# Two-layer transformer block on eight cores: a constant loaded first, an output projection in two parts, and the last feed-forward's norm and quantisation moved into the last head pair of attention

## What is computed

```python
def _L0_attn_ref(hidden_states, Wq, Wk, Wv, Wo):
    ...                                       # q, k: 16 heads of 16; v: 16 heads of 64
    A = jnp.tril(jnp.einsum('bhnf,bhmf->bhnm', taylor_exp(q), taylor_exp(k)))
    y = jnp.einsum('bhnm,bhme->bhne', A, v)   # divided by the row sums of A
    return y.transpose(0, 2, 1, 3).reshape(b, l, N_HEADS * V_DIM) @ Wo

def _L0_ffn_ref(x, w_gate, w_up, w_down):     # hidden 3072, int weights
    return (silu(x @ wg.T) * (x @ wu.T)) @ wd.T

def _L1_attn_ref(x, Wq, bq, Wk, bk, Wv, bv, Wo, bo, global_indices):
    ...                                       # 16 heads of 64, blocks of 64 tokens
    final = out_local + out_gk                # softmax over 3 blocks + softmax over 2 global blocks
    final = final.at[:, :, global_indices].set(out_rows)   # the two global blocks see all tokens
    return ctx @ Wo.T + bo

def _L1_ffn_ref(x, w1, conv_w, conv_b, w2):   # hidden 4096
    h = bit_linear(x, w1)                     # activations rounded to 8 bits by row, weights to -1, 0, 1
    h = silu(depthwise_conv1d(h))
    return bit_linear(h, w2)

x = x + _L0_attn_ref(_layernorm(x), ...)
x = x + _L0_ffn_ref(_layernorm(x), ...)
x = x + _L1_attn_ref(_layernorm(x), ...)
x = x + _L1_ffn_ref(_layernorm(x), ...)
```

## Time and profile before

| | |
|---|---|
| median of 3 runs | 2296.45 us (2292.74, 2296.45, 2488.86) |
| profiled execution, its own time | 2293.34 us |
| its span, slowest core (core 5) | 2291.8 us |
| spans of the eight cores | 2278.8 to 2291.8 us |
| PE busy | 1955.2 us (85%) |
| DVE, ACT, POOL busy | 1167.9, 1101.0, 28.7 us |

### The profile page before, as it was taken

The page is one execution under the profiler, slowest core; times in us unless marked ns, Lnnn a source line. Parts: engine busy times, 40 slices in busy tenths (PEclk is TensorE's granted clock), DMA queues, the critical chain, the costliest instruction groups (busy, mean ns, idle before and its releaser), DMA issues. The chain is left out here.

```text
span 2291.8 us, 35064 instructions; the slowest of 8 cores (2278.8 to 2291.8 us)
## 1 busy us (share of the span) xinstructions
PE 1955.2 (85%) x12314; PEld 911.1 (40%) x12314; DVE 1167.9 (51%) x2092; ACT 1101.0 (48%) x1994; POOL 28.7 (1%) x72
## 2 busy tenths in 40 slices
PE   3699999887899995999988888777893699979999
PEld 1334333323344442444444444444441344434444
DVE  2322656424535521521646666666556588875442
ACT  2477676754411100111225777677544788864221
POOL 0000000000000000000000000000000000000000
PEclk8799999868899997999999999788796699989999
DMA  7101545500087604622001000000101222241332
GB/s 191 30 1 38 168 162 169 119 2 1 1 212 225 215 28 83 203 63 46 1 1 29 11 11 11 11 11 2 38 1 75 83 74 74 74 136 57 111 118 85
DMA packets 64746, 170.12 MB, mean 74 GB/s; under 512 B 4416, under 2 KB 37184, under 8 KB 57664
## 3 DMA queue, kind: packets, MB, share of 16 engines
q1 hardware_dynamic: 58208, 134.31, 17.2%
q0 software_dynamic: 6368, 33.56, 8.4%
HBM read 167.85 MB, written 33.55 MB: 88 GB/s over the span
## 5 line engine op out<-in xcount | busy, mean ns | idle before, releaser
L671 PE MATMUL f0R<-lnT,wgu 128*128 128x512 bf16 x1536 | 336.0, 382 | 26.6 <-DMA wgu<-f0wgu_d 26.6
L431 ACT ACTIVATE a0bq<-a0S 128x1024 bf16<-128x1024 f32 (+1 forms) x320 | 268.8, 894 | 117.2 <-PE a0S L355 116.6
L671 PEld LDWEIGHTS f0R<-lnT,wgu 128*128 128x128 bf16 x1536 | 151.3, 99 | 210.9 <-issue 32.6
L706 ACT ACTIVATE f0si<-f0R 128x1024 bf16<-128x1024 f32 x48 | 49.2, 1025 | 386.6 <-PE f0R L671 386.6
L1305 PE MATMUL g1hp<-g1q1T,g1t 128*128 128x512 bf16 x1024 | 225.6, 381 | 5.4 <-DVE g1a L1425 4.0
L1329 PE MATMUL g1hp<-g1t,g1q1T 128*128 128x512 fp8e4 x1024 | 222.7, 381 | 2.1 <-ACT g1q1T L1380 2.1
L732 DVE TENSOR_TENSOR f0hT<-f0si,f0R 128x1024 bf16<-128x1024 bf16 x48 | 58.6, 1222 | 225.2 <-PE f0R L671 225.2
L1102 ACT ACTIVATE a1pt<-a1T 128x768 bf16<-128x768 bf16 (+2 forms) x152 | 118.6, 787 | 113.2 <-PE a1T L987 103.6
L372 PE MATMUL a0y<-a0bq,a0vv 128*64 128x512 bf16 (+3 forms) x640 | 128.4, 396 | 28.1 <-DVE a0yT L511 18.3
L1305 PEld LDWEIGHTS g1hp<-g1q1T,g1t 128*128 128x128 fp8e4 x1024 | 98.4, 98 | 132.4 <-issue 19.6
L1329 PEld LDWEIGHTS g1hp<-g1t,g1q1T 128*128 128x128 bf16 x1024 | 100.5, 98 | 124.1 <-issue 4.4
(11 more groups left out here) (189 smaller groups left out, 2947.9 us busy)
## 6 DMA issues: line engine op xcount, KB each, us to landing
a0wst<-g1w_d SPq DMA_DIRECT2D x64, 512.0 KB, 4.1
f0wst<-g1w_d SPq DMA_DIRECT2D x32, 1024.0 KB, 5.9
hs_scr<-g1hsp SPq DMA_DIRECT2D x32, 512.0 KB, 3.2
...
```

Source lines behind the costliest of these rows:

```text
L431: s.activation(bq[:, u % 4, :, n0:512], sS[:, u % 2, :, n0:512], AF.Square).then_inc(s_sq, 1)
L671: mm = t.matmul(R[:, k % 4, 512 * n2:512 * (n2 + 1)], wgu[:, cc % 3, x, j, :], lnT[:, j, t0 + 512 * n2:t0 + 512 * (n2 + 1)], start=(j == 0 ...
```

## The change

It has three parts.

1. Layer-0 attention's start: SP loads `a0qb` before x. The statistics run four tiles ahead instead of two, DVE also writes the negated mean (`neg`), and ACT itself makes `a0nb` from it; `a0lsc` has four buffers and the transposes use four PSUM banks.
2. Layer-0 output projection: `W` items carry a fourth field, the half of the heads. The halves over pairs 0 to 3 (32 items of 4 matmuls each, added to `xs`) are filled into pair 6 and the first two batches of pair 7, one or two in a batch; `finish` keeps the halves over pairs 4 to 7 (4 matmuls each). `wo` is loaded in two parts.
3. Norm and quantisation of the last feed-forward's input move into pair 7 of layer-1 attention: `finish(k)` there puts `Z` (row maximum and rounding of the tile before, DVE; back to bf16, now on POOL), `W`, `Q` (transposes two tiles back) and `N` (statistics on DVE, normalised tile on ACT). In pair 7, POOL takes over DVE's scaling in `X` and ACT takes over the write of `a1yT` in `V`. Part of the ternary weight `t1` (12 of 32 chunks) is loaded during attention, with a layout by chunk. The old stage in `emit_l1ffn` and its helper functions are gone.

```diff
@@ a0_order
+    first = [("W", ti, n2, 0) for ti in range(NT) for n2 in range(2)]
...
-        out.extend([("W", ti, 0), ("W", ti, 1)])
+        out.extend([("W", ti, 0, 1), ("W", ti, 1, 1)])
...
+        if 120 <= k < 142:
+            for _ in range(1 + k % 2 * (k < 140)):
+                out.append(first.pop(0))
@@ emit_l0attn, POOL and SP
-                g.wait_ge(s_pj, A0_PIECES * 4)
-                g.dma_start(wo[:, :, :], wo_d).then_inc(s_wo, 16)
+                for x in range(2):
+                    g.wait_ge(s_pj, A0_PIECES * (3 + x))
+                    g.dma_start(wo[x][:, :, :], wo_d[:, 4 * x:4 * x + 4, :]).then_inc(s_wo[x], 16)
...
+                sp.dma_start(qb[:, :], qb_d).then_inc(cstd, 16)
                 for g in range(8):
...
-                sp.dma_start(qb[:, :], qb_d).then_inc(cstd, 16)
@@ PE
-                        if ti >= 2:
-                            t.wait_ge(N1.ev, ti - 1)
-                        norm_pe_transpose(t, N1, lsc, ident, as_tiles(sS[:, ti % 2, 0, :]), ti)
+                        if ti >= 4:
+                            t.wait_ge(N1.ev, ti - 3)
+                        norm_pe_transpose(t, N1, lsc[:, ti // 2 % 2 * 2:, :], ident, as_tiles(lnp(ti)), ti)
...
-                        t.wait_ge(s_y, 29 + ti // 4)
-                        for j in range(ND):
+                        t.wait_ge(s_y, 29 + ti // 4 if x == 1 else 16)
+                        for j in range(4):
@@ ACT
-                            s.wait_ge(s_nb, ti // 2 + 1)
-                        if ti >= 2:
-                            s.wait_ge(N1.tp, ti - 1)
+                            s.drain()
+                            for i in range(ti, ti + 2):
+                                s.activation(nb[:, i:i + 1], N1.rstd[:, i:i + 1], AF.Copy,
+                                             scale=neg[:, i:i + 1])
+                            s.drain()
+                        if ti >= 4:
+                            s.wait_ge(N1.tp, ti - 3)
@@ a1_order
+    done = list(range(1, NT)) + [0]
+
+    def finish(k):
+        if k >= 1:
+            out.append(("Z", k - 1, done[k - 1]))
+        out.extend([("W", done[k], 0), ("W", done[k], 1)])
+        if k >= 2:
+            out.append(("Q", k - 2, done[k - 2]))
+        out.append(("N", k, done[k]))
...
         elif i < len(items) and m >= 5:
-            out += [("W", m - 4, 0), ("W", m - 4, 1)]
-    out += [("W", ti, n2) for ti in (13, 14, 15, 0) for n2 in range(2)]
-    return out
+            finish(m - 5)
+    for k in range(12, NT):
+        finish(k)
+    return out + [("Q", 14, done[14]), ("Z", 15, done[15]), ("Q", 15, done[15])]
@@ emit_l1attn, POOL: items X of pair 7, and Z
+                        g.wait_ge(s_rr, m + 1)
+                        if m < 16:
+                            for u in range(1 if m == 0 else 0, 2):
+                                lo = 64 if u == 0 else 0
+                                g.tensor_scalar(pp[:, m % 2, u, lo:lo + 192], pp[:, m % 2, u, lo:lo + 192],
+                                                rr[:, m % 2, 0, u:u + 1], None, ALU.mult)
+                                x = g.tensor_scalar(pp[:, m % 2, u, 256:384], pp[:, m % 2, u, 256:384],
+                                                    rr[:, m % 2, 1, u:u + 1], None, ALU.mult)
+                        else:
+                            x = g.tensor_scalar(pr_[:, :], pr_[:, :], rr[:, 2, 0, 0:1], None, ALU.mult)
+                        x.then_inc(s_p7, 1)
...
+                        g.tensor_scalar(q1c[:, k % 2, :], lx[k % 2].bitcast(I32)[:, :], am[:, ti:ti + 1],
+                                        1.0 / 127.0, ALU.mult, ALU.mult).then_inc(N.ap, 1)
@@ SP
+                sp.wait_ge(s_av, use(4, 0))
+                sp.dma_start(t1[:, 0:12, :, :], t_d[0, :, 0:12288].rearrange("p (c j d) -> p c j d", c=12, j=ND)
+                             ).then_inc(l_t1[0], 16)
@@ ACT: item N
+                        norm_act_rstd(s, N, k, ti, 1)
+                        s.drain()
+                        s.activation(nb[:, ti:ti + 1], N.rstd[:, ti:ti + 1], AF.Copy, scale=neg[:, ti:ti + 1])
+                        s.drain()
+                        if k >= 2:
+                            s.wait_ge(N.ap, k - 1)
+                        s.activation(lx[k % 2][:, :], xs[:, ti, :], AF.Identity, scale=N.rstd[:, ti:ti + 1],
+                                     bias=nb[:, ti:ti + 1]).then_inc(s_xh, 1)
@@ DVE: items N and Z
+                        v.drain()
+                        for hf in range(2):
+                            v.bn_stats(N.st6[:, k % 2, hf, :], xs[:, ti, 512 * hf:512 * (hf + 1)])
...
+                        v.wait_ge(s_xh, k + 1)
+                        v.tensor_reduce(am[:, ti:ti + 1], lx[k % 2][:, :], AX.X, ALU.max,
+                                        apply_absolute_value=True)
...
+                        v.tensor_scalar(lx[k % 2].bitcast(I32)[:, :], lx[k % 2][:, :], ra[:, ti:ti + 1], 127.0,
+                                        ALU.mult, ALU.mult).then_inc(s_qz, 1)
```

More of the change, by code:

```diff
@@ L215, in emit_l0attn @@
         lnT = place(nc, p + "lnT", 0, [128, ND, T], BF16)
-        wo = place(nc, p + "wo", 0, [128, ND, D], BF16)
+        wo = [place(nc, p + f"wo{x}", 48 - 48 * x, [128, 4, D], BF16) for x in range(2)]
         w0 = place(nc, p + "w0", 32, [128, 4, ND, 512], BF16)
@@ L241, in emit_l0attn @@
         N1, N2 = norm_state(nc, es, p + "n1"), norm_state(nc, es, p + "n2")
-        cst, cstd, s_nb = sem("cst"), sem("cstd"), sem("nb")
+        cst, cstd = sem("cst"), sem("cstd")
         l_x = [sem(f"x{g}") for g in range(8)]
         wq = [sem(f"w{g}") for g in range(4)]
-        s_wo = sem("wo")
+        s_wo = [sem(f"wo{x}") for x in range(2)]
         s_pj, s_pe = sem("pj"), sem("pe")
@@ L454, in _ @@
                 v.wait_ge(cst, 1)
-                v.wait_ge(l_x[0], 16)
-                for ti in range(2):
-                    norm_dve_stats(v, N1, xs, ti, ti)
+                for ti in range(4):
+                    stats(ti)
                 for it in order:
@@ L817, in emit_l1attn @@
     for it in order:
-        if it[0] in ("P", "W") or it[0] == "A" and it[2] == 0:
+        if it[0] in "PWQ" or it[0] == "A" and it[2] == 0:
             banked[it] = len(banked)
@@ L824, in emit_l1attn @@
     users = [it for _, it in users]
-    on_act = [it[0] == "P" and it[1] == "q" for it in users]
-    freed = [(a, sum(x == a for x in on_act[:n + 1])) for n, a in enumerate(on_act)]
+    by = ["n" if it[0] == "Q" else "q" if it[:2] == ("P", "q") else "p" for it in users]
+    freed = [(x, by[:n + 1].count(x)) for n, x in enumerate(by)]
     n_pre = 24
@@ L860, in emit_l1attn @@
         pr_ = place(nc, p + "pr", 136, [128, T], BF16)
+        lx = [place(nc, p + f"lx{i}", 120 - 8 * i, [128, D], F32) for i in range(2)]
+        q1c = place(nc, p + "q1c", 12, [128, 2, D], BF16)
+        neg = sb("neg", [128, NT], F32)
+        nb = sb("nb", [128, NT], F32)
+        am = sb("am", [128, NT], F32)
+        ra = sb("ra", [128, NT], F32)
         bo = sb("bor", [1, D], BF16)
@@ L1295, in _ @@
             def _(t):
-                for ti in range(NT):
-                    ln_pe_transpose(t, L, q1c, ident, tps, ti)
-                t.wait_ge(L.ev, NT)
-                t.wait_ge(l_t1, 16)
                 for c in range(NC):
+                    if c in (0, 12):
+                        t.wait_ge(l_t1[c // 12], 16)
                     if c >= 2:
```

237 lines of the change are left out of this document (106 added, 131 removed).

## The result

The changed kernel took 2243.5 us (median), the forecast was 2245. The ratio of its time to that of the kernel before is 0.978, with a 95% interval of 0.976 to 0.980. (Some executions had one die at a lower clock and took 2314 us and more, the 2488.86 in the table of before among them; they are left out of all medians, ratios and differences here.) The profiled execution took 2243.9 us, 49.4 less than the 2293.3 of before.

A forecast was written before the change was run, and what follows sets the result against it. PE was taken as nearly always busy except at the start and ahead of the last feed-forward, with a low clock in pair 6 and the output projection. 30 + 9 + 11 = 50 us gave 2245, range 2225 to 2267.

The forecast's parts named there:

- The start: First part of layer-0 attention: waits for `a0qb` and `a0nb` go, chunks shorten; 30 us gained, bounds 20 and 34.
- Rival 2: The start gives only its first wait, later chunks keep some 18 us each; 12 us worse, 2257; chance 0.10.
- Pair 6 and the output projection: Layer-0 attention: half the projection's matmuls filled into pair 6, whose higher clock pays two thirds; 9 us gained, bounds 3 and 15.
- Perhaps 0.5 more in the first batches of pair 7: Layer-0 attention, behind pair 6: a possible further gain of 0.5 us on top of 8.5.
- The last stage's way into pair 7: Layer-1 attention: norm and quantisation move into pair 7, 8.2 us per tile; 11 us gained, bounds -5 and 20.
- the step around the global rows: Pair 7 of layer 1, between twelfth and thirteenth tile, with the projection behind at the low clock: about 17 us.
- the table load at the first logarithm: Pair 7 of layer 1: one ACT function table load, counted at 1.3 us.
- pair 7's first five steps: Layer-1 attention: cost some 2 us, because ACT's share with the write of `a1yT` becomes the longest.
- POOL's price: Pair 7 of layer 1: scaling 640 columns a step taken as 1.1 us, `Z`'s 1024 as 1.6, steps hiding both.
- Rival 5: POOL becomes the bound of pair 7 at 13.3 us a tile; 77 us, 2322, slower than before; chance 0.03.
- Rival 4: Pair 7's exponential and logarithm need different ACT tables, each tile loading twice; 41 us worse, 2286; chance 0.04.
- Rivals 1 and 3: Longer loop or low PE clock in pair 7, 2265, chance 0.17; better clock in pairs 6, 7 and start, 2229, 0.09.

The follow-up runs named there:

- e1: The kernel before with only the issue of the constant `a0qb` moved ahead of the x loads; 2277.1 us, ratio 0.994.
- e12: The kernel of e2 with two buffers and two PSUM banks for the normalised tile and its transposition instead of four; 2256.0 us, ratio 0.984.
- e2: The kernel before with the whole new start of layer-0 attention and neither of the other two parts; 2255.9 us, ratio 0.985.
- e3: The changed kernel without its third part: layer-1 attention and last feed-forward as in the kernel before; 2244.5 us, ratio 0.980.
- e4: The kernel of e2 with 32 groups of four unused matmuls filled in at pair 6, output projection left whole in pair 7; 2263.9 us, ratio 0.988.
- e6: The changed kernel with the scaling of pair 7's first five steps back on DVE; uneven runs of 2236.9, 2241.3 and 2266.9 us, ratio 0.980.
- e11: The changed kernel with all of pair 7's scaling on DVE, `Z` behind the next tile's statistics and a tiny early Silu; 2220.0 us, ratio 0.969.
- e8: The changed kernel with one tiny unused Silu on ACT ahead of the last feed-forward's first evacuation; 2239.2 us, ratio 0.976.

## Why the prediction was right, and where it was not

The total came out (50 us forecast, 49.4 measured between the profiled executions), the three terms less so. That it is so close is in part luck: two terms gave somewhat more than forecast and the third less.

**The start, 30 forecast, 31 to 33 measured.** The mechanism is as written: first move at 37.6 (36 to 37 forecast), third chunk 11.8 behind the second (12 to 14), scores from 84.7. In the sum the fourth chunk stands with 1 us where the text in front of it has 2. e1 corrects the split: the constant alone is 12.6 us, not 8.8, because the statistics four tiles ahead, which I counted into the 36.5, push the first move back by some 5 us (32.6 in e1, 37.6 here); e12 shows that nothing of the rest is due to buffers. Rival 2 is out.

**Pair 6 and the output projection, 9 forecast, 10 to 11 measured.** Pair 6 took 62.5 us (65 forecast, and "62 to 68" to be seen), by the medians of e2 and e3 8 more instead of 9.5. "Perhaps 0.5 more in the first batches of pair 7" was too small: the clock handed on is worth 2.6 in pair 7 (e4). Off the diagonal the tiles lie 4.5 us apart, the last three too (4.7 forecast for both).

**The last stage's way into pair 7, 11 forecast, 4 to 8 measured.** The main sum held: 8.2 us a tile forecast, 8.12 measured, 152 us forecast, 152.2 on that core. It hid errors that cancel: the step around the global rows took 19.5 (17 forecast), the last three tiles 24.3 (27), and the table load at the first logarithm (1.3) is not there. The step that failed is the one on pair 7's first five steps, "some 2 us". It took 4.9. With DVE scaling, 2.4 of the 4.9 stay (19.9 against 17.5 in e6, and 19.9 again in e11), which fits the 2 for ACT's write of `a1yT`, though no run tests that write by itself. The other 2.4 are POOL's scaling: I had put its 1.1 us a step beside other work, but it took 2.8 us a step and part of that lay in the chain from scores to output. The second step that failed is a term put at nothing: the last feed-forward was left as it is, and it became 1.5 to 3 us longer. Of that, 1.3 us is the table load, which now stands where PE waits for it (e8); the rest stays open.

**POOL's price** is the number I had least of, and the bound was wrong on the side that costs. I took it from a memset and a select, 0.9 and 2.3 ns a column; it was 4.1 and 4.7 ns for 192 and 128 columns and 2.65 for 2048. From 192 and 128 columns one can estimate a fixed 0.25 us an operation and 2.7 ns a column (5.8 us for 2048, measured 5.4), so a step's four small operations pay the fixed part four times. Rows of DVE doing the very same operations were in the trace of before (0.27 and 0.25 us, and 0.75 for the global rows) and would have told what was given up: 1.0 us on DVE for 2.8 on POOL. The Trainium skill, GPSIMD Engine Reference, section 4.1, calls one-input work on this engine roughly line-rate; that does not hold here, where the 2048-column operation takes 7.2 times DVE's. The 1024 columns from int32 took 1.12 us, below my 1.6 and below the 2.2 that I had estimated by that page's section 3.1. Rival 5 decides from 11.5 us a step; POOL had 3.9 in one of 8.1, so it stayed far off.

**Rival 4, table loads:** the trace after has five, none of them between 1134.7 and 1767.0 us, so logarithm and attention's exponential were served by what was loaded. **Rivals 1 and 3:** the clock in pair 7 was lower (0.83 against 0.94), and the loop did not care (8.1 us a step at 0.79 as at 1.00), since DVE and ACT set it.
